# A gathered row enters PSUM by an ordinary fp32 matmul instead of a transpose-mode one

## The reference

```python
h = relu(layernorm(x))
edge_in = concat([h[src], h[dst], edge_weight1], axis=1)      # 212500 x 129
e = silu(edge_in @ eW1 + eb1)
e = silu(e @ eW2 + eb2)
agg = segment_sum(e, src, num_segments=12500)
node_in = concat([h, agg], axis=1)
out = x + (silu(node_in @ nW1 + nb1) @ nW2 + nb2)
```

## Time and profile before

| | |
|---|---|
| median of 3 runs | 3044.79 us (3040.09 to 11595.62) |
| span of the profiled execution | 3042.3 us; no other time is given for it |
| gathers, first and last | 788.7 us, 2998.1 us |
| busy, share of the span | PE 87%, PEld 68%, DVE 70%, ACT 53%, POOL 66% |
| mean of one L554 gather on POOL | 951 ns |
| mean of one L920, L929, L912 on DVE | 349, 291, 267 ns |
| mean of one L1435, L1437, L1443, L1449 on ACT | 591, 625, 687, 595 ns |

### The profile page before, as it was taken

One profiled execution on the slowest core, in us unless ns is written; L12 is line 12 of the kernel. 1 busy time (PEld: TensorE's weight loads), 2 busy tenths in 40 slices (PEclk: granted clock), 3 DMA queues, 4 the chain that ended last, 5 costly groups with the idle time before them and its releaser, 6 DMA issues.

```text
span 3042.3 us, 77490 instructions
## 1 busy us (share of the span) xinstructions
PE 2652.8 (87%) x21703; PEld 2068.1 (68%) x21704; DVE 2125.5 (70%) x7337; ACT 1601.7 (53%) x3366; POOL 2012.3 (66%) x2075
## 2 busy tenths in 40 slices
PE   7899999999688888888888888888888888888899
PEld 4555555555477777777777777777777777777776
DVE  8999999997566666666666666666666666666665
ACT  3677777777344444444444444444444444444455
POOL 1254444445677777777777777777777777777772
PEclk7999999999799999999999999999999999999999
DMA  3011111111222222222222222222222222222343
GB/s 94 20 40 27 39 28 39 34 34 30 48 59 59 60 57 59 59 60 59 58 59 59 60 60 58 58 60 59 59 59 59 59 59 58 58 59 55 77 120 103
DMA packets 366054, 171.78 MB, mean 56 GB/s; under 512 B 289494, under 2 KB 330126, under 8 KB 365934
## 3 DMA queue, kind: packets, MB, share of 16 engines
q0 software_dynamic: 69600, 123.49, 15.4%
q1 hardware_dynamic: 274142, 36.29, 7.8%
q10 hardware_dynamic: 22192, 10.53, 1.2%
HBM read 139.11 MB, written 31.04 MB: 56 GB/s over the span
## 4 chain that ended last, share of the span: by engine, by line
PE 81%; issue 11%; ACT 4%; DVE 3%; DMA 1%; POOL 0%; ACTq 0%; SPq 0%; DVEq 0%; POOLq 0%
PE bk L1208 16%; PE bk L1228 15%; PE bk L1219 13%; PE bk L1206 9%; PE bk L1196 5%; PE bk L1071 4%; PE bk L1217 3%; PE bk L1105 3%; PE bk L1137 2%; PE bk L1059 2%; PE bk L1060 2%; PE bk L1239 1%; ACT BIG L1354 1%; PE bk L1099 1%; PE bk L1274 1%
## 5 line engine op out<-in xcount | busy, mean ns | idle before, releaser
L554 POOL DMA_INDIRECT GA<-q_d,IX x1758 | 1671.5, 951 | 545.4 <-issue 533.3
L920 DVE SCALAR_TENSOR_TENSOR GA<-c_bc,EW,GA 128x128 f32<-128x128 f32 x1758 | 558.5, 349 | 432.7 <-DMA GA<-q_d,IX 429.2
L929 DVE TENSOR_TENSOR BIG<-bk,BIG 128x128 f32 x1758 | 511.4, 291 | 345.1 <-issue 156.4
L1206 PE MATMUL bk<-identf,GA 128*128 128x128 f32 x1758 | 501.2, 285 | 253.8 <-issue 240.3
L1208 PE MATMUL bk<-OHS,P 128*128 128x128 bf16 x5274 | 695.8, 225 | 0.1
L1443 ACT ACTIVATE ED<-bk,eb1c 128x512 f32<-128x512 f32 x440 | 302.1, 687 | 703.0 <-PE bk L1208 698.7
L1208 PEld LDWEIGHTS bk<-OHS,P 128*128 x5274 | 501.3, 96 | 111.3 <-issue 0.2
L1228 PE MATMUL bk<-ED 128*128 128x128 f32 x3516 | 504.7, 287 | 0.0
L519 POOL DMA_INDIRECT rec_d<-BIG,GA x208 | 246.8, 1187 | 376.9 <-issue 285.6
L1219 PEld LDWEIGHTS bk<-W,ED 128*128 128x128 f32 x3516 | 464.8, 193 | 24.3 <-issue 7.6
L1206 PEld LDWEIGHTS bk<-identf,GA 128*128 128x128 f32 x1758 | 247.5, 141 | 321.7 <-issue 297.2
(11 more groups left out here) (247 smaller groups left out, 2761.9 us busy)
## 6 DMA issues: line engine op xcount, KB each, us to landing
GA<-q_d,IX POOLq DMA_INDIRECT x1758, 2.5
q_d<-QS SPq DMA_DIRECT2D x14, 448.0 KB, 3.1
u_d<-QS ACTq DMA_DIRECT2D x98, 64.0 KB
OHS<-u_d SPq DMA_DIRECT2D x18, 256.0 KB, 3.1
rec_d<-ED SPq DMA_DIRECT2D x16, 220.0 KB, 9.6
RW<-rec_d SPq DMA_DIRECT2D x110, 32.0 KB
rec_d<-BIG,GA POOLq DMA_INDIRECT x208, 2.4
HT<-hT_d ACTq DMA_DIRECT2D x99, 32.0 KB
```

What stands on the lines that cost most here:

```text
L554: e.indirect_dma_start(G[k % 4 * U + u], None, q_d, bass.IndirectOffsetOnAxis(ap=IX[g // BG % 2][:, k * U + u:k * U + u + 1], axis=0))\
L920: ins = e.scalar_tensor_tensor(out=G[k % 4 * U + u], in0=c_bc[:, :], scalar=ew[:, w:w + 1], in1=G[k % 4 * U + u], op0=ALU.mult, op1=ALU.add)
L929: e.tensor_tensor(AGG[:, ds(v, P)], banks[6 + k % 2][:, u * P:(u + 1) * P], AGG[:, ds(v, P)], ALU.add).then_inc(s["ad"], 1)
L1206: e.matmul(z, G[k * U + u], identf[:, :], is_transpose=True, start=True, stop=False)
```

## The change

In step B of the main loop the matmul that brings in the gathered rows loses its transpose mode and becomes an ordinary fp32 matmul of the same operands: the rows, stationary, by the identity, moving. The product is the rows' transpose as before. The three bf16 matmuls that add to it, the waits, the buffers and the order of the steps stay. The transposes of the one-hots (`mA`) and those of the node layers stay in transpose mode.

```diff
                 for u, v in enumerate(vs[0:tiles(g)]):
                     z = banks[2][:, u * P:(u + 1) * P]
-                    e.matmul(z, G[k * U + u], identf[:, :], is_transpose=True, start=True, stop=False)
+                    e.matmul(z, G[k * U + u], identf[:, :], start=True, stop=False)
                     for q in range(3):
                         last = e.matmul(z, P3[q][:, ds(v, HF)], OHT[k % 2][:, u * P:(u + 1) * P],
                                         start=False, stop=(q == 2))
```

## The result

| | before | changed |
|---|---|---|
| median | 3040.68 us (6 runs, 3039.97 to 11595.62) | 3052.44 us (6 runs, 3049.32 to 3053.9) |
| ratio | | 1.0038, 95% interval 1.0028 to 1.0048 |
| span of the profiled execution | 3042.3 us | 3050.4 us |

The changed kernel is 11.8 us slower, 0.4% and so within 2%, and the interval of the ratio lies wholly above 1. The profiled execution of the changed kernel took 3052.19 us, 1.8 us more than its span.

A forecast was written before the change was run, and what follows sets the result against it. POOL's gathers were taken to bound the main loop (added cost 0), PE the tail (10.4 - 0.6 = +9.8 us). 3042.3 + 9.8 + 2.5 = 3054.6 us, ratio 1.003, own range 3048 to 3064 us.

The forecast's parts named there:

- POOL paces the loop: Main loop, 416 groups: POOL's gathers, 5.013 us a group, hide PE's added work; sum 0.
- The tail pays: From group 416 on PE is the bound and added time is paid; +9.8 us.
- the 3010 named: Sign at the end of the gathers: POOL's last gather comes before 3010 us.
- Price per tile in the tail: Tail, step B: one more record per tile costs PE +0.111 us, between 0.055 and 0.124.
- I cost the loads at nothing: PE's weight loads: the longer fp32 loads, 193 ns, are hidden behind bf16 matmuls and add nothing.
- rival (c): Loop and tail: fp32 loads not hidden, 0.136 us exposed, price 0.247 us per tile, about 3236 us; chance 0.08.
- The seam: Tail, L1196 to L1228: the first fp32 load behind bf16 transposes cost nothing visible; evidence against exposed loads.
- Number of tiles in the tail: From group 416 on, 94 tiles pay 10.4 us, less one pause of 0.60 us.
- PE's need in the loop: Main loop: PE needs 4.339 + 0.09 + 0.444 = 4.873 us a group against POOL's 5.013; 0.14 us left.
- a third of 0.675: Sign in the loop: PE's idle time before L1206 cut to about a third; 0.675 us idle per group before.
- (b): Main loop: PE becomes the bound by a little if a tile's price exceeds 0.146 us; 3064 to 3100 us; chance 0.10.
- (d): Whole kernel: nothing to be seen, ordinary form in one record or hidden in a tail gap; 3040 to 3048 us; chance 0.05.

The follow-up runs named there:

- the loop alone: Against the kernel before: ordinary matmuls in groups 0 to 415, transpose mode kept in the tail; 3040.38 us, ratio 0.9997.
- few gathers: Kernel before and changed kernel, each with one gather per group and one plain transfer for three tiles: 2621.02 us (transpose mode) and 2730.33 us (ordinary).
- Tail alone: Against the kernel before: transpose mode kept in groups 0 to 415, ordinary matmuls in the tail; 3052.28 us, ratio 1.004.
- the alternating kernel: Changed kernel with the ordinary matmul first in tiles 0 and 2 of a group, last in tiles 1 and 3; 3051.96 us, ratio 1.004.

## Why the prediction was right, and where it was lucky

**POOL paces the loop: right.** The same 1117 gathers in the window, the loop alone at 0.9997, and the fall to 4.00 us a group with few gathers show it. The page's "PE 87%" and a chain with 81% of PE would have promised up to 6% for 0.44 us in 416 groups.

**The tail pays: right.** Tail alone has a ratio of 1.0040 beside the 1.0038 of the whole change. POOL's waits for PE went from 7 to 14, and the last gather came at 3004.7 us, before the 3010 named.

**Price per tile in the tail: under-sized.** The term was +0.111 us (0.055 to 0.124), measured 0.60/4 = 0.15. The second record cost the 0.111. What failed is "I cost the loads at nothing": an ordinary fp32 matmul behind a short bf16 one costs 0.055 us more, in three of four tiles, by the reading above because its load is uncovered. In that reading the mechanism of rival (c) exists, at 0.055 us instead of 0.136. The seam that I read as evidence against it, from L1196 to L1228, was misread: with steps of 0.111 us eight records of L1228 are 0.89 us, as L1219's are, and the row has 0.95. The 0.06 us more are of the size of the uncovered load, inside the piece and not as a gap ahead of it. L1219 doesn't show it, since the 512 columns of L1217 (0.22 us) stand ahead of it. This reading of the old rows was made afterwards; what is measured is the position's effect in the alternating kernel.

**Number of tiles in the tail: over-sized.** I counted 94 tiles from group 416 on, less one pause of 0.60 us, and wrote that PE does the node layers from there; `inner` begins with group 418. PE is full only from group 421 on, when `outer` and `turned` have joined. Ahead of it the changed kernel still pauses, in the chain of its groups 416 to 421:

```profile
2892.21 0.36 issue
...
2902.53 0.29 issue
```

Of the groups from 421 on, 18.5 by 0.60 us are 11.1 us, and tail alone gave 11.15. The two chains bear it out: from L1196 of group 421 to the end of the span it is 134.0 us before (from 2908.28) and 144.5 us changed (from 2905.91), 10.5 us more. My 10.4 - 0.6 = 9.8 us came near by two errors that cancel: a price a quarter too small, a count a quarter too large. The start was off too: the profiled kernel before had a stretch at a clock of 0.75 near the tail's entry, which the profiled changed one lacks (1.00 from 2886.2 to 2893.0 us), and the first median was 4.1 us above that of more runs. The forecast of +9.8 us stands beside +11.8. That 3054.6 us lies above 3052.44 although the difference was forecast too small is the work of that start.

**PE's need in the loop: over-sized by far.** I added 4 x 0.111 = 0.444 us to a busy time of 4.339 us per group and found 0.14 us of slack. Measured, the busy time rose by 31.5/279.25 = 0.113 us, PE stayed idle for 0.56 us per group and not for a third of 0.675, and with few gathers, on another chip, PE managed a group in 4.23 us. The prediction named the reason and then didn't use it: right behind a wait, instructions come more slowly than the array takes them. Of the group of the earlier trace rows that begins at 2010.18, the pieces behind its gathered tiles in the kernel before are:

```profile
2011.92 0.38 PE bk L1196 x4
2012.30 0.99 PE bk L1228 x8
...
2014.39 0.75 issue
```

Step B took 1.74 us and the whole 4.21 us. In the changed kernel B takes 1.96 us and the whole 4.23 us: the tile grew from 0.37 to 0.45 us, the four bf16 transposes shrank from 0.38 to 0.22 us and L1228 from 0.99 to 0.95. While the array works longer in B, the instructions behind it catch up, and the time comes back in A and D. The few-gathers chains have the same: 0.61 us of array work per group in a stretch without pauses, 0.23 us on average. That instruction supply is what spreads these pieces is argued from where the time comes back; no experiment measured it alone.

**Rivals.** (b), PE as the bound by a little, needed a price of 0.146 us per tile in the loop, and even at the tail's 0.15 the loop didn't feel it, because PE's need was 4.23 us and not 4.87. Its upper end is refuted: the ordinary form does take four bf16 steps (0.222 us), but the transpose-mode one takes two (0.111), not one. The Trainium skill's four times for FP32 (TensorE: Matmul & The Clock Gate, "Terms") isn't seen here; the factor is two. (c) is refuted in its price and its place, (d) by the counts and by 6.59 us. The clock was full (1.00) from 1400 to 2800 and from 2935 to 2965 us in both kernels, so the rule on transpose mode and the clock that the prediction quotes had next to nothing to act on. On the slower chip it was 0.89 with the transpose-mode matmul alone in B and PE busy for 734.07 of 1000 us, and 1.00 with ordinary matmuls added (875.83). But the few-gathers kernel in transpose mode has 1.00 there too, with PE busy for 967.92, so transpose mode by itself doesn't lower it; no run parts the mode of the matmuls from their amount further than that.

## What to carry to other kernels

Ask of each stage which engine's stream has no gaps: here POOL, with 66% on the page, paced 416 of 440 groups, and a doubled matmul on the 87% engine was free there and cost its full price in the 18 groups in which PE was full. A busy time measured while an engine waits often isn't its need: part of it, by the account above, is the slow restart after each wait, and added array work fills that first. For a step's price divide a piece of the chain by its count and compare lines with each other: 0.95 against 0.89 us for eight equal matmuls was the sign of the 0.055 us that the prediction lacked.

## What was not expected of the hardware

- Two more chips take 3511 to 3558 us for the kernel before, 15 to 17% more than 3041, with equal gather lengths; in the one profile of that kernel there, a median 2.88 us pass from the end of B to its reader, instead of 0.03, and the granted clock of its loop is 0.89 instead of 1.00. With one gather and one plain transfer in a group in place of four gathers the same chip has 0.04 us. What holds the signal up stays open.
- An ordinary fp32 matmul of 128 columns takes 0.22 us of PE behind other fp32 work and 0.28 us behind bf16 matmuls of 128 columns; in transpose mode it is 0.11 to 0.12 us in either place.
